# The first maxima of an attention sequence turned in another PSUM bank and earlier, two router reads moved ahead of the layer norm's statistics, and x loaded two sequences further ahead

## The reference

```python
x = L0_attn_u
xn = _layernorm(x)
x = x + _L0_attn_ref(xn, ...) + _L0_ffn_ref(xn, ...)   # Mamba block; 8 experts, top 2, inner 512, and a shared expert
xn = _layernorm(x)
x = x + _L1_attn_ref(xn, ...) + _L1_ffn_ref(xn, ...)   # causal attention; 8 experts, top 2, inner 128, and a shared expert
```

```python
scores = jnp.einsum('bqhd,bkhd->bhqk', q, k) * scale
scores = jnp.where(causal[None, None], scores, -jnp.inf)
attn = jax.nn.softmax(scores, axis=-1)
out = jnp.einsum('bhqk,bkhd->bqhd', attn, v).reshape(b, t, d)
return out @ w_o
```

## Time and profile before

| | |
|---|---|
| runs | 1422.0, 1423.79, 1427.99 us; median 1423.79 |
| the profiled execution | 1419.87 us, its span 1418.1 us |
| TensorE | 1320.0 us busy, 93% |
| VectorE | 911.0 us busy, 64% |
| ScalarE | 511.0 us busy, 36% |
| GpSimd | 655.5 us busy, 46% |
| TensorE's granted clock, mean | 0.983 of 2.4 GHz |
| chain that ended last | TensorE 80%, VectorE 10%, GpSimd 4%, issue 4% |

### The profile page before, as it was taken

How to read it: one execution, slowest core, us unless ns; L and a number is a source line. 1 busy time by engine, 2 the same in 40 slices (tenths; PEclk the granted TensorE clock), 3 DMA queues, 4 the chain that set the end, 5 groups by cost and what they waited for, 6 DMA issues and landing times.

```text
span 1418.1 us, 30111 instructions
## 1 busy us (share of the span) xinstructions
PE 1320.0 (93%) x10668; PEld 1039.8 (73%) x10684; DVE 911.0 (64%) x3115; ACT 511.0 (36%) x1096; POOL 655.5 (46%) x801
## 2 busy tenths in 40 slices
PE   7989999999999999899998899999998978999986
PEld 6878889888888889666666556666565646888875
DVE  4566534555655654589998778888888752333356
ACT  2122122222222222333333455555555534444331
POOL 2456423333333332455553145454544454677772
PEclk9999999999999999999999999999999979999998
DMA  9921941111111114500000101111010001223377
GB/s 339 213 52 31 87 102 46 52 46 46 46 50 49 46 46 156 183 1 0 0 0 9 60 24 46 36 35 42 29 46 9 10 2 50 93 101 104 113 236 243
DMA packets 77446, 102.05 MB, mean 72 GB/s; under 512 B 13021, under 2 KB 65260, under 8 KB 77312
## 3 DMA queue, kind: packets, MB, share of 16 engines
q1 hardware_dynamic: 59200, 62.35, 16.4%
q0 software_dynamic: 18112, 37.93, 8.2%
HBM read 64.26 MB, written 35.98 MB: 71 GB/s over the span
## 4 chain that ended last, share of the span: by engine, by line
PE 80%; DVE 10%; POOL 4%; issue 4%; DMA 1%; ACT 1%; another core or an unknown queue 1%; SPq 0%; DVEq 0%; POOLq 0%
PE score L1886 46%; PE mixed L1886 17%; PE side L1886 11%; DVE score L1725 3%; PE side L2130 2%; POOL y_rows L843 2%; DVE ARENA L1733 1%; PE side L1896 1%; PE mixed L2340 1%; DVE WGU L1725 1%; POOL ARENA L808 1%; POOL XN L835 1%; DVE stats L1166 1%; DVE X L1843 1%
## 5 line engine op out<-in xcount | busy, mean ns | idle before, releaser
L835 POOL DMA_INDIRECT XN<-xn_rows,slot_tok x106 | 108.6, 1024 | 219.3 <-PE side L2130 192.6
L1725 DVE CUSTOM_DVE_ANT_0 score<-score,future_b 128x128 f32<-128x128 f32 (+1 forms) x512 | 167.7, 390 | 56.1 <-PE score L1886 55.7
L843 POOL DMA_INDIRECT y_rows<-sh_gu,slot_row x144 | 144.7, 1005 | 89.4 <-ACT sh_gu L1036 50.9
L871 POOL TENSOR_SCALAR_AFFINE_SELECT ARENA<-ARENA 128x256 f32<-128x256 f32 x256 | 104.0, 430 | 164.3 <-ACT ARENA L1076 163.6
L1886 PE MATMUL score<-xT,HT 128*128 128x128 f32 x912 | 167.0, 275 | 0.0
L1076 ACT ACTIVATE ARENA<-score 128x768 f32<-128x768 f32 x128 | 104.0, 812 | 140.8 <-PE score L1886 140.6
L1886 PE MATMUL score<-ARENA 32*128 32x256 f32 (+1 forms) x2048 | 128.2, 357 | 27.6 <-DVE ARENA L1733 10.7
L773 POOL DMA_INDIRECT lists<-token_no,w_in x128 | 125.6, 981 | 33.4 <-issue 30.4
L1886 PEld LDWEIGHTS score<-xT,HT 128*128 128x128 f32 x912 | 133.9, 192 | 0.0
L808 POOL TENSOR_TENSOR ARENA<-tri_le,DT 128x1024 bf16<-128x1024 bf16 x48 | 90.2, 1895 | 87.6 <-PE mixed L1886 34.5
L1036 ACT ACTIVATE sh_gu<-mixed 128x256 f32<-128x256 f32 x144 | 55.4, 385 | 207.5 <-PE mixed L1886 207.5
(11 more groups left out here) (306 smaller groups left out, 2764.8 us busy)
## 6 DMA issues: line engine op xcount, KB each, us to landing
WGU<-in_gu SPq DMA_DIRECT2D x8, 1024.0 KB, 14.9
WGU<-y_rows SPq DMA_DIRECT2D x32, 256.0 KB, 3.4
ARENA<-y_rows SPq DMA_DIRECT2D x32, 256.0 KB, 3.9
xn_rows<-XN SPq DMA_DIRECT2D x24, 256.0 KB
X<-in_u SPq DMA_DIRECT2D x16, 256.0 KB
ARENA<-in_dn SPq DMA_DIRECT2D x8, 512.0 KB
x_parked<-X SPq DMA_DIRECT2D x4, 1024.0 KB
X<-x_parked SPq DMA_DIRECT2D x4, 1024.0 KB
```

Source lines behind the costliest of these rows:

```text
L835: x["got"][j % ring].mark(eng.indirect_dma_start(XG[j % ring], None, xn_rows[l], bass.IndirectOffsetOnAxis(slot_tok[:, col:col + 1], 0)))
L843: x["out"][j % YRING[l]].mark(eng.indirect_dma_start(y_rows[g], bass.IndirectOffsetOnAxis(slot_row[:, col:col + 1], 0), yo(l, j), None))
L871: ins = eng.affine_select(out=m, in_=m, compare_op=ALU.is_ge, fill=0.0, base=0, pattern=[[0, 2], [1, P]], channel_multiplier=-1)
L1725: ins = eng.tensor_tensor_reduce(s, s, future, -1.0, BIG, ALU.add, ALU.min, NM[:, c, j, at:at + 1])
```

## The change

`turn_maxima(b, 0)` and the reads of `shift(b, 0)` use bank 6, while those of j = 1 stay in bank 5. `turn_maxima(b, 0)` goes ahead of `scores(0, now(2), held(3))` and waits for ScalarE's copy of bank 6 (`oc` of 2 d.n) in place of `add_out`. The wait for `add_out` goes to `keys(a, 0)`, the next that writes bank 5. On VectorE `shift(b, 0)` goes ahead of `maxima(b, 2, 0)`, and `stats_stage(c)` behind the read of the logits or ranks. In the front, SyncE issues `load_x` of 7, 8 and 9 in the turn n = 1 and of n + 8 from n = 2 on.

```diff
+    def maxima_bank(j):
+
+        return bank[6 - j]
+
@@ sync, the front
         for n in range(NSEQ):
-            if n + 6 < NSEQ:
-                load_x(n + 6)
+            for ahead in range(n + (6 if n < 2 else 8), min(n + (7 if n < 1 else 9), NSEQ)):
+                load_x(ahead)
@@ vector, shift
-                ins = stt(q, bank[5][:, 0:SEQ], head_mask[:, 1 - e:2 - e], q, ALU.mult, ALU.add)
+                ins = stt(q, maxima_bank(j)[:, 0:SEQ], head_mask[:, 1 - e:2 - e], q, ALU.mult, ALU.add)
@@ vector, attention
             if b:
+                shift(b, 0)
                 maxima(b, 2, 0)
-                shift(b, 0)
-            if c and c.n > 1:
-                stats_stage(c)
             if a:
                 if a.v == 1:
                     logits_stage(1, a.i)
                 if a.v == 0 and not is_first(a):
                     rank_sums(1, a.i - 1)
+            if c and c.n > 1:
+                stats_stage(c)
+            if a:
                 if a.n == SPLIT + 3:
                     list_done(1)
@@ tensor, turn_maxima
-                ins = eng.transpose(bank[5][:, c * P:(c + 1) * P], NM[:, c, j, :], ident[:, :])
+                ins = eng.transpose(maxima_bank(j)[:, c * P:(c + 1) * P], NM[:, c, j, :], ident[:, :])
@@ tensor, attention
+            if b:
+                if d:
+                    A["oc"].wait(eng, 2 * d.n)
+                turn_maxima(b, 0)
             scores(0, now(2), held(3))
-            if b:
-                if o:
-                    A["add"].wait(eng, o.n)
-                turn_maxima(b, 0)
@@
             if a:
                 queries(a, 0)
+                if o:
+                    A["add"].wait(eng, o.n)
                 keys(a, 0)
```

## The result

| | before | after |
|---|---|---|
| median of 9 runs | 1422.28 us | 1414.86 us |
| ratio, 95% interval | | 0.9938 (0.9913 to 0.9964) |
| span of the profiled execution | 1418.1 us | 1413.0 us |

The kernel became 7.4 us faster; the forecast was 1413.9 us, 9.9 faster, with a range of 1407 to 1420. Single runs of one kernel lie up to 13 us apart, and by the interval the difference of the two medians is good to about 3.6 us. The profiles are needed to say where the time went.

What follows compares the result with a forecast made beforehand. In the attention neither TensorE nor VectorE alone bounds; TensorE waits in series for VectorE's order. Attention 7.0 + 3.7 = 10.7 us gained, front 0.8 lost: -9.9 from 1423.8 gives 1413.9 us, range 1407 to 1420.

Steps and rivals of the forecast that it cites:

- two serial waits: Attention: TensorE waits in series for VectorE's shift (10.5 us), then its rank read (4.6) or logits copy (2.9).
- Rival (a): Attention: the rest of VectorE's queue bounds, so moved reads only move waits to the maxima; 1419.1 us, chance 0.17.
- Rank turn: Attention: scores 0.4 us and queries 1.1 us earlier, 1.0 us per turn carried on; 7 turns, 7.0 us.
- Slots take 1.55, so the next maxima start at 916.5: Rank turn on VectorE: next maxima start at 916.5 instead of 917.23, ending at 917.85, before TensorE needs them at 917.9.
- Logits turn: Attention: scores of group 3 at 938.6 instead of 939.21, 0.6 us gained per turn; 3.7 us with the first turn's loss.
- The first turn: Attention: scores now stand behind the transposes' 1.26 us wait for maxima; a loss of 0.5 us.
- rival (d): Attention: TensorE's clock; one more stretch at 1.2 GHz could come, 4 us less gained, 1417.9 us, chance 0.08.
- Front: x loads ahead of sequence 2's store delay it 1.4 us, 0.6 of it slack; 0.8 us lost.
- 0.52 MB more ahead of it is 1.4 us later: Front, SyncE's queue: at 382 GB/s the added x loads delay the store of sequence 2 by 1.4 us.
- the front's length moves by more than 3 us: Front: a sign that the prediction is wrong, as would be turns staying above 22.8 us.
- The stall at 72.91: Front: VectorE's 8.96 us with no engine behind it, read as late code; effect taken as zero, between -8.96 and +8.96.
- rival (b): Front: the stall at 72.91 shrinks, half of 8.96 gained besides, 4.5 us; 1409.4 us, chance 0.13.

Runs made afterwards that it cites:

- e9: The whole change measured once more against before, on another chip: 1411.09 us, ratio 0.9929.
- e3: Against before, only the early transposes and shift in bank 6; statistics in their old place, x loads as before: 1412.40 us, ratio 0.9936.
- e4: Against before, only the statistics moved behind the reads of logits and ranks: 1413.51 us, ratio 0.9939.
- e5: Against e2, the old order of transposes, scores, shift and maxima in the first turn alone: 1411.07 us, ratio to before 0.9923.
- e2: Against before, the attention's change alone, without the moved loads of x: 1411.71 us, ratio 0.9922.
- e10: The attention's change alone (e2) measured once more against before, on the chip of e9: 1406.85 us, ratio 0.9915.
- e1: Against before, only the loads of x moved: 1425.59 us, ratio 1.0014.
- e6: Against e2, early transposes stay in bank 5 and wait for VectorE's add of the projected output: 1424.91 us, ratio to before 1.0020.
- e7: Against the whole change, the seven 512 KB loads issued in turn n = 3 instead of n = 1: 1416.71 us, ratio to before 0.9953.
- e8: Candidate: e5 plus e7's edit of the 512 KB loads, x loaded as before: 1408.12 us, ratio to before 0.9917.
- e11: The candidate (e8) measured once more against before, on the chip of e9 and e10: 1405.18 us, ratio 0.9895.

## Why the prediction was right

- **The verdict** held: 7.4 us gained by the first 9 runs, 8.6 in e9's group, against 9.9 forecast. Both numbers stand on sums of terms, some of which were off and cancelled.
- **The two serial waits** were the mechanism, and by the length of the turns each was worth its part: e3 and e4. The medians of e3 and e4 do not separate the parts. Rival (a) did not come true: scores of group 3 came 0.98 us earlier. Part of what went did become a wait for maxima, though (5.6 us before, 12.5 after, 3.7 of it one wait in the last turn).
- **Rank turn: 1.0 us forecast, 0.73 measured.** The steps hold to 0.1 us until the scores of group 3, which came 0.98 us earlier counted from the start of the turn (5.67 behind the transposes, forecast 5.6); the transposes occupy 0.33 us between starts, not 0.27. The step that was off is "Slots take 1.55, so the next maxima start at 916.5": the slots took 1.75 (918.16 to 919.91), their first instruction 0.46 instead of 0.22 us. The next maxima then bound TensorE by the 0.19 us in the row at 921.42. Why that instruction is longer was not tried.
- **Logits turn: 0.6 forecast, 0.76 measured.** The turned logits were there earlier than I had put it: VectorE copied them 2.80 us behind the transposes, not 3.0 (938.00), so statistics and maxima followed sooner.
- **The first turn: a loss of 0.5 forecast, 2.7 measured.** I had counted the scores behind the wait, not the clock that falls behind a longer idle time. I had that as rival (d), at 4 us and a chance of 0.08; it should have been in the sum. The rows beside e5's show it. In the next turn before was at 1.2 GHz for a while (granted 0.93, 23.47 us) and after was not (1.00, 22.05), which gives about 0.7 us back.
- **The last turns: nothing forecast, 2.6 us gained** between 1110.77 and 1164.43 before (53.66 us) and the same places after (51.10). The granted clock tells them apart: 0.73 in the last of these turns before, 0.88 after, since before was at 1.2 GHz twice there and after once. Whether the change did this is open. The same code took 53.6 us in e2 and 51.1 in e10; but all three profiles without any part of the gain (before, e1, e6) took 53.2 us or more, and eight of the ten others 51.0 to 51.2.
- **Attention in all:** forecast 10.7, in the profile 12.8 - 2.7 = 10.1. That they agree is partly luck: some 3 us of it (0.7 in the second turn, 2.4 in the last) are the clock, which the forecast had at nothing, and they cancel the first turn's 2.7. The seven rank turns gave 5.7 with the second turn's clock in it, where 7.0 were forecast.
- **Front: a loss of 0.8 forecast; 2 to 4 by three pairs of medians, none clear of noise.** The step that was off is "0.52 MB more ahead of it is 1.4 us later" at 382 GB/s. The store wait rose by 4.7 us. SyncE issued that store at 45.95 instead of 44.09, 1.9 us later, and the norm that needs it followed 13.1 us behind the issue instead of 10.1. A likely reason, not tested by itself, is that the queues did not keep the fast rate: between 50 and 60 us loads and stores together moved only 146 GB/s (129 before):

```profile
42.00:50.00 8.00, 8.00 (x54) 6.69 (x53) 6.86 (x30) 1.64 (x4) 4.98 (x6) 1.00 1.08 380
50.00:60.00 10.00, 6.05 (x34) 4.95 (x33) 1.10 (x4) 0.77 (x2) 4.58 (x5) 0.98 1.15 146
```

In the pair of before and after these 4.7 us cost nothing in the end, since the stall behind them went: both stood level at 108 us. The sign "the front's length moves by more than 3 us" was not met at 133 us (1.4), and was at the start of the attention (4.1).
- **The stall at 72.91** had been left at zero between -8.96 and +8.96. In the whole change VectorE stood there 5 us less, which is rival (b)'s effect, and the longer store wait used it up. A stall of VectorE or ScalarE with no engine behind it is in every one of these profiles, at other places and of other sizes (the longest of each 3.6 to 10.6 us). That it is code arriving late remains a reading: no run took code away. So the prediction's "the trace disagrees with its 8.96 us" is not shown either.

**Open.** Why e3 and e4 each came within 2 us of both parts together, when their turns show half. The spread of single runs is as large as the difference. The front's stalls are one part of it, and the clock is another: from the first turned maxima to the last TensorE was at 1.2 GHz for about 24 us in before, 27 in e1, e2 and e7, 20 in e6, 17 in after, e4, e5 and e8 to e11, and 14 in e3. That fits e2's attention, which had shorter turns and was no shorter than e3's and e4's. What sets these stretches was not tested.

## What to carry to other kernels

When an engine shows several waits for one other engine in one turn, look at the order of that engine's queue: what releases the bound engine goes first, what has slack (here statistics, needed 3 us later) goes under the next matmuls. An order can only change when the operands are free, so look for a bank or buffer that is idle just then; here the same order in the old bank gave nothing. Reading further ahead can cost when the loads stand in one queue in front of a store that someone waits for (4 to 5 us of wait here, 2 to 4 us of time by medians), and it gained nothing here, where no row showed a wait for a load. When TensorE's idle time moves, read the granted clock over the whole stage before crediting a turn's gain: what the old first turn saved, later turns took back.

## What the runs showed of the hardware

- In the attention's first turn TensorE's clock was at 1.2 GHz behind an idle time of 2.76 us and stayed there for 9 us or more, with 8.27 of 9 us busy (after). In the seven profiles with this idle time the stretch was some 7 to 10 us long, in the six with 1.26 us there 3 to 7. The turn grew by 2.7 us, the idle time by 1.5.
- The same kernel does not always get the same clock: e2 was at 1.2 GHz for about 27 us of its attention and took 364.5 us, e10 for 17 and took 360.3.
- With loads and stores of x's rows alternating in SyncE's queue, all queues together moved 126 to 150 GB/s (50 to 60 us, before, after, e1 and e2), where 380 to 382 had been moved from 42 to 50 us, at a DMA share of 1.15 to 1.24 against 1.08 and 1.09. Whether the stores, the size of the rows or the waits between issues made the difference was not separated.
- Single executions of one kernel lie 3 us (e11, 6 runs) to 21 us (before, 24 runs) apart, and the first store of rows, 215 us into a program that is the same to there, lay at 210.6 to 222.2 us in seven profiles. A difference of 3 us needs either many runs or a row that shows it.
